# Softplus in a conv, Mamba and mixture-of-experts kernel: the rounding of 1+e found on ScalarE instead of GpSimd

## The reference, cut to what matters

```
dbc = xs @ x_proj_w.T
dt  = softplus(dbc[..., :16] @ dt_proj_w.T + dt_proj_b)
dA  = exp(dt[..., None] * A)
dBu = dt[..., None] * Bm[:, :, None, :] * xs[..., None]
hs  = associative_scan(...)(dA, dBu)
```

## Time and profile before

| | |
|---|---|
| median of 3 runs | 5216.6 us (5200.36 to 5223.23) |
| profiled execution, its own time | 5213.57 us |
| its span | 5211.8 us |
| busy share of the span | TensorE 84%, VectorE 77%, GpSimd 75%, ScalarE 64% |
| mean granted TensorE clock | 0.937 |

### The profile page before, as it was taken

The page is one execution under the profiler, slowest core; times in us unless marked ns, Lnnn a source line. Parts: engine busy times, 40 slices in busy tenths (PEclk is TensorE's granted clock), DMA queues, the critical chain, the costliest instruction groups (busy, mean ns, idle before and its releaser), DMA issues. The chain is left out here.

```text
span 5211.8 us, 70837 instructions
## 1 busy us (share of the span) xinstructions
PE 4357.3 (84%) x21206; PEld 1771.7 (34%) x21206; DVE 4025.3 (77%) x6073; ACT 3334.8 (64%) x5405; POOL 3922.9 (75%) x4937
## 2 busy tenths in 40 slices
PE   3577788888888888888889888789888888888887
PEld 1233333333333333333333333333333333332332
DVE  2278887888877887888878888788878788788771
ACT  1255566767666766676767676667666676676665
POOL 1277787888877887888878888788878888788772
PEclk9588999999999998999999999899999999999997
DMA  2365564555555654555545555455555555554420
GB/s 66 72 148 141 134 140 114 138 131 136 125 118 118 140 132 106 135 136 129 133 113 134 131 133 127 109 137 136 130 116 131 128 135 127 115 117 106 98 62 5
DMA packets 255558, 623.33 MB, mean 120 GB/s; under 512 B 105268, under 2 KB 170676, under 8 KB 255028
## 3 DMA queue, kind: packets, MB, share of 16 engines
q1 hardware_dynamic: 255156, 618.60, 51.5%
HBM read 540.85 MB, written 77.65 MB: 119 GB/s over the span
## 5 line engine op out<-in xcount | busy, mean ns | idle before, releaser
L1193 POOL TENSOR_TENSOR hc<-hs,cb 128x448 f32<-128x448 f32 x1792 | 2030.5, 1136 | 751.6 <-DVE hs L1030 726.9
L1030 DVE TENSOR_TENSOR_SCAN hs<-dtb,state,ps 128x448 f32<-128x448 f32 x1792 | 2047.4, 1143 | 105.8 <-issue 1.8
L1020 DVE TENSOR_TENSOR ps<-ps,bb 128x448 f32<-128x448 f32 x1792 | 1098.7, 613 | 443.9 <-PE ps L687 437.9
L865 ACT ACTIVATE dtb<-dtb,decay 128x448 f32<-128x448 f32 x1792 | 1086.2, 657 | 198.4 <-DMA dtb<-dt_scratch 193.5
L687 PE MATMUL ps<-dux,pick 128*128 128x448 bf16 x3584 | 1049.1, 374 | 164.6 <-DVE hs L1030 102.5
L907 ACT ACTIVATE hg<-ps,be 128x448 f32<-128x448 f32 x896 | 520.1, 631 | 430.5 <-PE ps L751 429.0
L687 PE MATMUL ps<-duz,pick 128*128 128x448 bf16 x1792 | 649.2, 362 | 0.0
L751 PE MATMUL ps<-xn,we 64*128 64x448 f32 x1792 | 583.3, 621 | 53.5 <-ACT hg L907 53.0
L687 PEld LDWEIGHTS ps<-dux,pick 128*128 128x128 bf16 x3584 | 264.6, 99 | 865.4 <-issue 527.8
L734 PE MATMUL ps<-h,w 96*128 96x448 bf16 x896 | 313.0, 385 | 212.5 <-ACT rz L896 86.3
L699 PE MATMUL ps<-hc,gather 128*32 128x448 f32 x3584 | 454.2, 580 | 8.7 <-POOL hc L1193 8.4
(11 more groups left out here) (175 smaller groups left out, 6277.2 us busy)
## 6 DMA issues: line engine op xcount, KB each, us to landing
dtb<-dt_scratch SPq DMA_DIRECT2D x448, 896.0 KB, 6.6
slab<-h_scratch SPq DMA_DIRECT2D x168, 290.0 KB, 8.1
dt_scratch<-sp SPq DMA_DIRECT2D x112, 224.0 KB, 2.0
h_scratch<-h2p SPq DMA_DIRECT2D x168, 112.0 KB
h<-h_scratch SPq DMA_DIRECT2D x56, 336.0 KB, 4.1
h_scratch<-h1s SPq DMA_DIRECT2D x56, 232.0 KB, 3.9
xw<-xn_scratch SPq DMA_DIRECT2D x112, 112.8 KB, 2.6
xw<-xn_scratch SPq DMA_DIRECT2D x112, 112.5 KB, 2.7
```

Of the source, the lines that this page charges most:

```text
L865: A.activation(a, a, ACT.Exp, scale=decay[k % 2][:, i:i + 1]).then_inc(a_ok, 1)
L1020: V.tensor_tensor(bank, bank, bb[:, k % 2, :], ALU.mult).then_inc(bu_ok, 1)
L1030: V.tensor_tensor_scan(rev(hs[:, n % RH, :], d), rev(dtb[i // 4][:, i % 4, :], d), rev(bank, d), state[:, d, i:i + 1], ALU.mult, ALU.add). ...
L1193: P_.tensor_tensor(hc[:, n % 8, :], hs[:, n % RH, :], cb[:, k % 2, :], ALU.mult).then_inc(hc_ok, 1)
```

## The change

ScalarE forms y = 1+e in the tile that part 1 of dt*u will use later (`dux[:, kk % 2, 1, :]`), and then 1-y in place: two Identity activations with a bias (`lost`, called at slot 0 of a step, at the end of ScalarE's work of that slot). GpSimd's `soft_ym` goes; `soft_log` adds 1-y from that tile instead of subtracting (1+e)-1. Two counters are new: `dt_y` between the two activations, and `dt_r`, for which `soft_log` waits. `lost` also waits until TensorE has read the tile's older content (`bu_ps`).

```diff
@@ ScalarE
+                    def lost(kk):
+                        y = dux[:, kk % 2, 1, :]
+                        if run and kk >= 2:
+                            act.wait_ge(bu_ps, DS * (kk - 1))
+                        if n1(kk) >= 0:
+                            act.wait_ge(dt_e, n1(kk) + 1)
+                        A.activation(y, sp[:, 0, :], ACT.Identity, bias=1.0).then_inc(dt_y, 1)
+                        act.wait_ge(dt_y, n2(kk) + 1)
+                        A.activation(y, y, ACT.Identity, bias=1.0, scale=-1.0).then_inc(dt_r, 1)
@@ ScalarE, loop over slots
+                            if i == 0 and second_half(k):
+                                lost(k + 1)
@@ GpSimd
-                    def soft_ym(kk):
-                        pool.wait_ge(sp_ch, 3 * n2(kk) + 1)
-                        P_.tensor_scalar(sp[:, 0, :], sp[:, 0, :], 1.0, -1.0, ALU.add, ALU.add).then_inc(sp_ch, 1)
-
                     def soft_log(kk):
-                        pool.wait_ge(sp_ch, 3 * n2(kk) + 2)
-                        P_.tensor_tensor(sp[:, 2, :], sp[:, 2, :], sp[:, 0, :], ALU.subtract).then_inc(sp_ch, 1)
+                        pool.wait_ge(sp_ch, 2 * n2(kk) + 1)
+                        pool.wait_ge(dt_r, n2(kk) + 1)
+                        P_.tensor_tensor(sp[:, 2, :], sp[:, 2, :], dux[:, kk % 2, 1, :], ALU.add).then_inc(sp_ch, 1)
@@ GpSimd, loop over slots
-                            if i == 1:
-                                soft_ym(k + 1)
```

More of the change, by code:

```diff
@@ L377, in build @@
         dtb_in = [sem(f"dtb_in{j}") for j in range(4)]
-        dt_e, dt_l, sp_ch, dt_ok, dx_ok = (sem(n) for n in ("dt_e", "dt_l", "sp_ch", "dt_ok", "dx_ok"))
+        dt_e, dt_l, dt_y, dt_r, sp_ch, dt_ok, dx_ok = (sem(n) for n in
+            ("dt_e", "dt_l", "dt_y", "dt_r", "sp_ch", "dt_ok", "dx_ok"))
         bu_ps, bu_ok, a_ok, h_ok, st_ok, hc_ok, y_acc, gated, o_ps, o_rd, st0 = (sem(n) for n in
@@ L1203, in soft_le @@
                         P_.tensor_tensor(sp[:, 2, :], sp[:, 2, :], sp[:, 0, :], ALU.add).then_inc(sp_ch, 1)
-                    def soft_ym(kk):
-                        pool.wait_ge(sp_ch, 3 * n2(kk) + 1)
-                        P_.tensor_scalar(sp[:, 0, :], sp[:, 0, :], 1.0, -1.0, ALU.add, ALU.add).then_inc(sp_ch, 1)
                     def soft_log(kk):
-                        pool.wait_ge(sp_ch, 3 * n2(kk) + 2)
-                        P_.tensor_tensor(sp[:, 2, :], sp[:, 2, :], sp[:, 0, :], ALU.subtract).then_inc(sp_ch, 1)
+                        pool.wait_ge(sp_ch, 2 * n2(kk) + 1)
+                        pool.wait_ge(dt_r, n2(kk) + 1)
+                        P_.tensor_tensor(sp[:, 2, :], sp[:, 2, :], dux[:, kk % 2, 1, :], ALU.add).then_inc(sp_ch, 1)
                     def soft_dt(kk):
-                        pool.wait_ge(sp_ch, 3 * n2(kk) + 3)
+                        pool.wait_ge(sp_ch, 2 * n2(kk) + 2)
                         P_.tensor_tensor(sp[:, 1, :], sp[:, 2, :], sp[:, 1, :], ALU.add).then_inc(dt_ok, 1)
```

## The result

The changed kernel takes 5490.8 us (median of 4 runs, 5487.4 to 5522.0), the kernel before 5218.7 us: ratio 1.054, 95% interval 1.050 to 1.059. The forecast was 5243 us in a range of 5190 to 5285. The sign is right, the size is wrong by a factor of nine (29 us forecast, 272 measured), and the time lies far outside the range.

A forecast was written before the change was run, and what follows sets the result against it. No engine was taken to fill the span; what counts is the few places where somebody waits. 5213.6 + 0 (GpSimd) + 29.4 (ScalarE, odd step) + 0 (ScalarE, even step) = 5243 us, range 5190 to 5285.

The forecast's parts named there:

- Part 1: GpSimd without soft_ym: the saved wait for `xntd` is handed back behind dt's late DMA; gain 0, at most 52 us.
- The rival that had the mechanism: GpSimd, earlier by 1.7 us, stops blocking VectorE at L1077; VectorE wins 55 us, 5188 us in all; chance 0.07.
- Part 2: Odd step: ScalarE's new pair ahead of `h1s` delays TensorE by 1.13 us in 31 waits; 29.4 us, bounds 0 and 35.
- Part 3: Even step: ScalarE's new pair falls between gelu pairs, mostly into idle time; 0 to 5 us, taken as 0.
- The clock rival: Longer TensorE stalls at L734 and `h1s` make its clock fall more often; 49 us more, 5292 us; chance 0.13.

The follow-up runs named there:

- e7: Kernel before without soft_ym, nothing in its place, and GpSimd waiting in slot 6 of odd steps until VectorE's deviations are written; ratio 1.007.
- e2: Kernel before without GpSimd's soft_ym and with nothing in its place, so the rounding of 1+e is not corrected; ratio 1.037.
- e6: Changed kernel with GpSimd waiting in slot 6 of odd steps until VectorE's deviations are written; ratio 1.021.
- e4: Changed kernel with GpSimd's soft_ym kept, its result unused, in the even steps only; ratio 1.045.
- e1: Changed kernel with GpSimd's soft_ym kept in all steps, its result unused; ratio 1.020.
- e11: e1 with 7 small zero-weight matmuls on TensorE ahead of the stream that waits for h1s; ratio 1.010.
- e12: Kernel before with 7 small zero-weight matmuls in slot 14, ahead of the job where TensorE waits 1.86 us for ScalarE; 5152.5 us, ratio 0.989.
- e15: Changed kernel with zero-weight matmuls ahead of TensorE's waits at three places: late gelus (8), h1s (7), slot 14 (7); ratio 1.023.
- e10: Changed kernel with 8 small zero-weight matmuls ahead of TensorE's first ring job in the stall at the late gelus; ratio 1.031.
- e13: Changed kernel with zero-weight matmuls behind TensorE's waits at three places: late gelus (8), h1s (7), slot 14 (7); ratio 1.064.
- e14: Changed kernel with `lost` in slot 1, GpSimd's slot 6 wait in odd steps, and 7 zero-weight matmuls behind TensorE's slot 14 wait; ratio 1.022.

## Why the prediction was wrong

**Part 1, the step that failed.** "I take the gain of part 1 as 0" was read from the even step alone. There it held: the spread of dt is as late as before, and the wait moved from `xntd` to L896. Details were off. `xntd` came 0.5 us earlier, not up to 1.7, for GpSimd now waits 1.16 us for a scan; and the wait for L896 grew by 15 us, not by some 50. GpSimd was also not quite without idle time there in before: it waited 0.29 us for `h2p` behind `soft_le`. The spread was issued 5.00 us after `arrange` had left the queue (2631.72 to 2636.72), in before 4.67. But the multiply is taken from the odd step too, and the forecast never followed GpSimd through it. Some five slots further on, GpSimd now arrives earlier beside VectorE's subtraction at L1069. This alone costs 3.0 points by e7 against e2 and 3.3 by e6 against after, 160 to 170 us; by e4 against e1 it is 2.6.

**The rival that had the mechanism.** The hold of GpSimd on VectorE stood in the text as a possible gain at L1077, at 0.07, with the remark that a VectorE operation could be "blocked anew". Both happened. L1077 fell from 82.3 to 19.0 us, and no run shows that this gave anything back; L1069 rose by 94 us, with ScalarE's square, two gelus and TensorE behind it. I had priced the relieved operation by its own length and given the newly held one no price. The Trainium skill ("SBUF — State Buffer", section on the two separate sides) says that a VectorE operation with two inputs in SBUF, as this one is, and a GpSimd operation that reads SBUF exclude each other on a shared port, and that whichever starts first has it for the whole instruction. The rows here agree with the exclusion and show it lasting longer than one instruction: 2.56 us, across four of GpSimd's with no gap.

**Part 2, right in its mechanism.** The wait for `h1s` grew by 33.0 us in the same 31 waits, where 29.4 were forecast. The pair costs what was said, and no table load was added (L991 x225, as in the earlier trace rows):

```profile
L991 ACT ACT_TABLE_LOAD x225 | 288.7, 1283 | 4.0
...
L943 ACT ACTIVATE dux<-dux 128x448 f32<-128x448 f32 x112 | 64.6, 577 | 3.6
L941 ACT ACTIVATE dux<-sp 128x448 f32<-128x448 f32 x112 | 63.7, 568 | 0.0
```

The term was mis-sized as a whole all the same. e1, which is nearly part 2 alone, lost 2.0% or 100 us, and with the clock held up there (e11) 1.0% or 50 us. Some 20 us of that are not the `h1s` wait's own. I did not trace them; in a few periods of e1 VectorE's subtraction is held as well (mean 0.64 us instead of 0.51). The upper bound of this term, 35 us, was too low: it allowed for no clock.

**Part 3, not contradicted.** TensorE's waits for gelus at its first expert matmuls are 28.0 us in after and 32.6 in before. No run takes the even step's pair away by itself.

**The clock rival, right in kind and too small.** It got 0.13 and +49 us, "half such a stretch" in 35 periods. (The range went up to 5285 us, so it took in 42 of these 49 us, not half of them.) The chance should have been higher on the evidence that was there. Counted in TensorE's records from 690 to 4900 us, in before 57 stalls of 1.5 to 2.0 us were followed by a fall of the granted clock within six us 35 times, and 213 stalls of 0.6 to 1.0 us only 23 times. The forecast itself took one stall from 0.8 to 1.9 us and another from 0.69 to 2.0, out of the second group into the first, and never counted. In the wider band of 1.5 to 2.6 us, before has 66 stalls, 41 of them followed by a fall, and after has 128, with 97.

**How much is clock.** e12 bought 60.6 us by 121 us less low time, 0.5 us for each. By that price the 386 us that after has more are 190 us of its 272. By e15 against e12, where the low time is equal, 3.4 points remain, and the clock's share is 2.0 of 5.4, about 105 us. Both are estimates from the runs, and it stays open where between them the share lies: e15 bought 3.1 points, 164 us, by 502 us less low time, only 0.33 us for each, and fillers may also cost something of their own.

## What to carry to other kernels

Work taken from an engine with idle time is not free to take. Follow its stream to the next place where it now runs beside another engine's operation, and price what is held there by everything queued behind it; e6 shows that a wait at the right place can be worth 3%. Count TensorE's stalls by length before costing a change: in these runs, filling a stall of 1.9 to 2.2 us bought back 1.1 us each in e12 (53 stalls filled), 1.4 in e11 (35) and 2.6 in e10 (46), so that much such a stall had cost beyond its own length. If a stall can't be removed, matmuls that change nothing, issued ahead of its wait, are worth trying (e12), and behind the wait they only cost (e13, e14).

## What the runs showed of the hardware

- A VectorE operation of 0.42 to 0.51 us, from SBUF to SBUF with two inputs, took 2.56 us under four back-to-back GpSimd operations and ended with the last of them, in 46 of 56 periods. VectorE's operation on `ps` just before, at 2591.56, took 0.61 us beside `by_c`; 0.63 in the earlier trace rows.
- A GpSimd operation of 1.7 us less moved that hold from a 112x4 operation (82.3 us in all) to a 112x256 one, where it cost 3%.
- A stall of TensorE of 1.86 us, with 0.43 us busy of 2, was followed by a clock of 0.53 for six us. The same 1.86 us with 14 short matmuls in it were followed by 1.00.
